# One fused rotation, attention and quantised-FFN kernel: six short steps put in other places of VectorE's, ScalarE's and TensorE's queues

## The reference, cut to what matters

```
a, ang = amplitudes ** dt, frequencies * dt          # one pair per sequence and feature
x' = rotate(x; a*cos(ang), a*sin(ang))
q, k, v = x' @ W_qkv.T (16 heads of 16); k = layernorm(k)
S = gamma_h * S + v_t k_t^T; y_t = S q_t             # decaying linear attention over the 64 tokens
x1 = x + y @ W_o.T
s = tanh(x1 @ W1 + b1) @ v                           # one score per token
p = softmax(masked s over the 64 tokens), mask by the sequence's type
pooled = (p @ x1) / count of unmasked tokens
g = clip(round(pooled / sx)), weights rounded to 8 bits by the largest |w| of each row
out = x1 + dequant(round(silu(g @ Wg) * (g @ Wu)) @ Wd)
```

## Time and profile before

| | us |
|---|---|
| median of 3 runs (275.56 to 279.0) | 275.73 |
| the profiled execution | 275.67 |
| its span in the trace | 273.9 |
| TensorE busy (matmuls) | 254.1 (93%) |
| VectorE busy | 226.4 (83%) |
| ScalarE busy | 183.3 (67%) |
| GpSimd busy | 145.9 (53%) |

### The profile page before, as it was taken

How to read it: one execution, slowest core, us unless ns; L and a number is a source line. 1 busy time by engine, 2 the same in 40 slices (tenths; PEclk the granted TensorE clock), 3 DMA queues, 4 the chain that set the end, 5 groups by cost and what they waited for, 6 DMA issues and landing times.

```text
span 273.9 us, 8463 instructions
## 1 busy us (share of the span) xinstructions
PE 254.1 (93%) x3529; PEld 174.6 (64%) x3529; DVE 226.4 (83%) x483; ACT 183.3 (67%) x325; POOL 145.9 (53%) x144
## 2 busy tenths in 40 slices
PE   5799999989799799989999999998989999998994
PEld 5568788679578677957977977875634434443331
DVE  4879678499779958995996876888888999999994
ACT  5796463562369557858768358437699999838991
POOL 6998693871790395069169233005012779850570
PEclk9999999999999999999999999999999999999999
DMA  5991306204400800390291142040009489000277
GB/s 161 347 276 42 117 2 222 91 0 175 138 2 2 278 33 2 122 244 6 56 288 26 33 146 39 9 149 6 0 34 183 114 221 366 7 0 0 80 257 279
DMA packets 30310, 31.20 MB, mean 114 GB/s; under 512 B 12928, under 2 KB 20672, under 8 KB 30272
## 3 DMA queue, kind: packets, MB, share of 16 engines
q1 hardware_dynamic: 30272, 30.66, 37.4%
HBM read 19.48 MB, written 8.42 MB: 102 GB/s over the span
## 4 chain that ended last, share of the span: by engine, by line
PE 53%; DVE 26%; ACT 12%; issue 5%; DMA 1%; POOL 1%; DVEq 0%; ACTq 0%
PE psum L901 10%; PE psum L1290 6%; DVE arena L1461 5%; PE psum L941 4%; PE psum L1309 3%; PE psum L926 3%; PE psum L1062 3%; ACT silu L864 2%; PE psum L1008 2%; PE psum L1068 2%; PE psum L1063 2%; PE psum L1064 2%; PE psum L1069 2%; ACT silu L846 2%; PE psum L1051 2%
## 5 line engine op out<-in xcount | busy, mean ns | idle before, releaser
L1461 DVE TENSOR_TENSOR arena<-psum,xq_mem 128x512 f32<-128x512 f32 x64 | 39.6, 681 | 3.8 <-PE psum L926 3.7
L560 POOL TENSOR_TENSOR xT_lo<-arena,xT 128x512 fp32r<-128x512 f32 x14 | 17.5, 1273 | 45.4 <-ACT xT L689 45.4
L1290 PE MATMUL psum<-xq_mem,guT 128*128 128x512 bf16 x152 | 33.9, 379 | 0.2
L1290 PEld LDWEIGHTS psum<-xq_mem,guT 128*128 128x128 bf16 x152 | 14.3, 98 | 19.4 <-DVE arena L1675 1.8
L1686 DVE TENSOR_REDUCE h_max<-arena 128x1 f32<-128x1024 f32 (+1 forms) x24 | 25.9, 1123 | 0.2
L846 ACT ACTIVATE silu<-psum,gu_x 128x1024 f32<-128x1024 f32 (+1 forms) x24 | 24.4, 1026 | 2.1 <-PE psum L1290 1.1
L689 ACT ACTIVATE xT<-arena 128x512 fp32r<-128x512 f32 x14 | 8.1, 623 | 22.6 <-PE psum L901 20.9
L941 PE MATMUL psum<-arena 64*32 64x128 f32 x1024 | 19.4, 274 | 1.5 <-DVE arena L1461 1.5
L671 ACT ACTIVATE arena<-psum,pmask 128x512 f32<-128x512 f32 x32 | 20.2, 684 | 0.4 <-PE psum L1069 0.4
L1309 PE MATMUL psum<-arena,dT 128*128 128x512 bf16 x80 | 18.9, 380 | 1.2 <-DVE arena L1745 0.6
L926 PE MATMUL psum<-arena 32*64 32x128 f32 x1024 | 19.7, 278 | 0.1
(11 more groups left out here) (247 smaller groups left out, 721.4 us busy)
## 6 DMA issues: line engine op xcount, KB each, us to landing
arena<-in_x SPq DMA_DIRECT2D x9, 512.0 KB, 3.8
x_dram<-arena SPq DMA_DIRECT2D x8, 512.0 KB, 4.0
pooled<-x_dram SPq DMA_DIRECT2D x8, 512.0 KB, 5.3
out<-pooled SPq DMA_DIRECT2D x15, 256.0 KB, 2.1
xin<-in_x_t SPq DMA_DIRECT2D x7, 512.0 KB, 4.4
cs_rows<-cs_dram SPq DMA_DIRECT2D x12, 256.0 KB, 5.3
pooled<-in_w_qkv_t SPq DMA_DIRECT2D x3, 256.0 KB, 5.0
pooled<-in_w_down SPq DMA_DIRECT2D x1, 704.0 KB, 7.8
```

What stands on the lines that cost most here:

```text
L560: pool.tensor_tensor(xT_lo[:, k, :], xrotT[:, k, :], xT[:, k, :].bitcast(F32), ALU.subtract).then_inc(xl_ok, 1)
L1290: mm = pe.matmul(in_order(o[:, 512 * half:512 * half + 512], 2 * n + half), gT[i][:, v, c, :], xq_rows(2 * n + half, c), start=(c == 0), s ...
L1461: dve.tensor_tensor(dec[:, c, r, :, :], bank[S_BANK[r]].rearrange("q (n k) -> q n k", n=PP), two_heads, ALU.mult).then_inc(dec_done, 1)
```

## The change

Six edits, all of order or of place:

1. VectorE: `scale_v` of each group stands behind `softmax_weights`, `scales` and the clip factors instead of ahead of them.
2. VectorE: `gu_largest(0)` of group 1 stands ahead of `softmax_scores` (it stood behind `sums_copy`); `gu_largest(1)` and `down_largest` of groups 2 and 3 stand ahead of `sums_copy` (they stood behind it).
3. ScalarE writes the first 8 columns of sine and cosine to PSUM (banks 2 and 3) and the other 24 to SBUF: four activations instead of two; VectorE's L1398 and L1399 read them in PSUM; the other columns' products wait for `trig_ok` at 4.
4. TensorE: the turn of the cosine table stands behind `scores(0, 0)` instead of ahead of `squares(0, 0)`, and goes to bank 2.
5. ScalarE: the copy to `cs_T` stands behind both pairs of query copies and both exponents. `hidden_weights` waits for it instead of `scores(0, 0)`.
6. TensorE's matmuls without a use at the start (`keep_clock`) write bank 0 instead of bank 3.

```diff
@@ ScalarE, start
-            act.activation(ang[:, 4, :], ang[:, 2, :], ACT.Sin).then_inc(trig_ok, 1)
-            act.activation(ang[:, 5, :], ang[:, 3, :], ACT.Sin).then_inc(trig_ok, 1)
+            first, rest = slice(0, 2 * PP), slice(2 * PP, NPAIR)
+            act.activation(bank[2][:, first], ang[:, 2, first], ACT.Sin).then_inc(trig_ok, 1)
+            act.activation(bank[3][:, first], ang[:, 3, first], ACT.Sin).then_inc(trig_ok, 1)
+            act.activation(ang[:, 4, rest], ang[:, 2, rest], ACT.Sin).then_inc(trig_ok, 1)
+            act.activation(ang[:, 5, rest], ang[:, 3, rest], ACT.Sin).then_inc(trig_ok, 1)
@@ ScalarE, ahead of the loop
-            act.wait_ge(cs_tr, 1)
-            act.activation(cs_T[:, :], bank[4][0:2 * NPAIR, 0:P], ACT.Copy).then_inc(csT_ok, 1)
             for c in range(DC):
                 q_copies(0, c)
                 act.wait_ge(dec_arg, c + 1)
                 act.activation(decay[:, HC * c:HC * c + HC, :], ..., ACT.Exp).then_inc(dec_exp, 1)
+            act.wait_ge(cs_tr, 1)
+            act.activation(cs_T[:, :], bank[2][0:2 * NPAIR, 0:P], ACT.Copy).then_inc(csT_ok, 1)
@@ TensorE
             def scores(g, c):
-                    pe.wait_ge(csT_ok, 1)
             def hidden_weights():
+                pe.wait_ge(csT_ok, 1)
-            pe.wait_ge(cs_ok, 2)
-            pe.wait_ge(csr_ok, 2)
-            pe.transpose(bank[4][0:2 * NPAIR, 0:P], cs[:, :, :]..., ident[:, :]).then_inc(cs_tr, 1)
             squares(0, 0)
...
                 scores(g, 0)
                 if g == 0:
+                    pe.wait_ge(cs_ok, 2)
+                    pe.transpose(bank[2][0:2 * NPAIR, 0:P], cs[:, :, :]..., ident[:, :]).then_inc(cs_tr, 1)
                     pe.wait_ge(wl_ok, 2)
@@ VectorE, start
-            dve.tensor_tensor(cs[:, 1, first], a_pow[:, first], ang[:, 4, first], ALU.mult)
-            dve.tensor_tensor(cs[:, 0, first], a_pow[:, first], ang[:, 5, first], ALU.mult).then_inc(cs1_ok, 1)
+            dve.tensor_tensor(cs[:, 1, first], a_pow[:, first], bank[2][:, first], ALU.mult)
+            dve.tensor_tensor(cs[:, 0, first], a_pow[:, first], bank[3][:, first], ALU.mult).then_inc(cs1_ok, 1)
...
             dve.wait_ge(pow_ok, 2)
+            dve.wait_ge(trig_ok, 4)
@@ VectorE, loop over g
                 decays(g, 0)
-                for p in range(PP) if g else (2, 3, 0, 1):
-                    scale_v(g, p)
                 if 2 <= g < G - 1:
                     softmax_weights(c - 1)
...
                 elif g == G - 1:
                     softmax_weights(c - 1)
+                for p in range(PP) if g else (2, 3, 0, 1):
+                    scale_v(g, p)
...
                 decays(g, 1)
...
+                if g == 1:
+                    gu_largest(0)
                 if g:
                     softmax_scores(c)
...
                     softmax_sums(c)
-                    sums_copy(g + 1)
-                    if g < 3:
-                        gu_largest(g - 1)
+                    if g == 2:
+                        gu_largest(1)
                     elif g == 3:
                         down_largest()
+                    sums_copy(g + 1)
                     y_odd(g, 0)
```

More of the change, by code:

```diff
@@ L1097, in project_v @@
                               v_mm if p % 2 else None, False)
-            keep_clock(14, bank[3][:, 0:P], ident[:, :], ident[:, :])
+            keep_clock(14, bank[0][:, 0:P], ident[:, :], ident[:, :])
             pe.wait_ge(cs1_ok, 1)
@@ L1109, in _ @@
                 last.then_inc(xT_tr, 1)
-                keep_clock(1, bank[3][:, 0:P], ident[:, :], ident[:, :])
+                keep_clock(1, bank[0][:, 0:P], ident[:, :], ident[:, :])
             pe.wait_ge(wk_ok, 1)
@@ L1126, in _ @@
             project_x(0, Q_BANK, 0, 0, q_mm)
-            pe.wait_ge(cs_ok, 2)
-            pe.wait_ge(csr_ok, 2)
-            pe.transpose(bank[4][0:2 * NPAIR, 0:P], cs[:, :, :].rearrange("p k n -> p (k n)"), ident[:, :]).then_inc(cs_tr, 1)
             squares(0, 0)
@@ L1144, in _ @@
                 if g == 0:
+                    pe.wait_ge(cs_ok, 2)
+                    pe.transpose(bank[2][0:2 * NPAIR, 0:P], cs[:, :, :].rearrange("p k n -> p (k n)"), ident[:, :]).then_inc(cs_tr, 1)
                     pe.wait_ge(wl_ok, 2)
```

## The result

| | before | after |
|---|---|---|
| median, us | 275.72 (4 runs) | 268.0 (4 runs, 267.99 to 268.05) |
| ratio of after to before | | 0.971, 95% interval 0.9669 to 0.975 |
| span in the trace, us | 273.9 | 266.3 |

The change makes the kernel 7.7 us faster. The forecast was 268.6, in 267.0 to 271.8. Some executions are longer at a lower granted clock (the kernel before ran up to 279.0 us here, and in the first experiments six of its 17 took about 278.7 at 0.987 or 0.988), and the ratios still contain such ones, so that they can differ by 0.3% from what the medians give.

The account below looks back on a forecast made before the run. The prediction took TensorE to bound the kernel, with 6.07 us of holes in groups 1 to 4 from late VectorE and other steps. Loop 6.4, cosine turn 0.5 and sines 0.2 made 7.1: 275.67 to 268.6 us, range 267.0 to 271.8.

Parts of the forecast that it names:

- Total: Whole kernel: loop, cosine turn and sines in PSUM together save 7.1 us, giving 268.6 us.
- Sum of the loop: Groups 1 to 4: 5.8 us from holes that go, 6.6 from groups as dense as group 5; 6.4 taken.
- its upper way: Loop estimate in which groups 1 to 4 become as dense as group 5: 6.6 us.
- Edit 1, hold and gap: VectorE's softmax steps, 0.9 us, fit the 1.08 us before L560; TensorE's 1.64 us hole goes in groups 2 and 3.
- Edit 1, cover of `scale_v`: In group 2 `scale_v` ends at 68.95, TensorE's pooling wants it at 69.9: 0.95 us to spare.
- Edit 2 and "the two edits are worth their sum only together": Moved maxima remove `yT` waits: 0.89 us in group 1, 0.4 and 0.25 in 2 and 3; otherwise earlier TensorE waits longer.
- Cosine turn: At the start, moving TensorE's cosine turn behind the scores takes 0.56 us off the path; gain 0.5, between 0.2 and 0.6.
- Sines in PSUM: At the start, L1398 falls from 0.95 to 0.15 us, but L1406 is held by GpSimd's casts; gain 0.2 us.
- A: TensorE meets another wait (held softmax steps, late `scale_v` or `yT`): 271.8 us, or 270.2 with three quarters kept; chance 0.21.
- B: GpSimd isn't the cause and VectorE's long operations stay long; only maxima and start count: 274 us; chance 0.07.
- C: L560 starts ahead of the softmax steps even in the new order, holding VectorE and delaying `scale_v`: 278 us; chance 0.04.
- D: Groups 1 to 4 fall under the forecast floor and L1406 isn't held: 267 us; chance 0.06.

Follow-up runs that it names:

- the first experiments: Follow-up runs made after the change was measured, each with the kernel before run beside it; its medians there were 276.13, 275.68 and 275.61 us.
- old_order_late_low: Kernel before, VectorE order untouched, with GpSimd's L560 of groups 2 to 6 waiting until that group's softmax weights are made: 271.21 us, 271.27 in a second trace.
- scale_v_late: Changed kernel with two unread 128x1024 reductions ahead of `scale_v` in groups 2 to 6: 272.88 us.
- only_order: Kernel before with only the softmax steps and scales moved ahead of `scale_v`: 271.3 us.
- only_maxima: Kernel before with only the weight maxima moved into other VectorE gaps: 269.8 us.
- rot_psum: Changed kernel with ScalarE's half of the rotation of group 0 also in PSUM, leaving L1408 one SBUF operand: 267.32 us.
- maxima_slip: Kernel before with only the maxima moved, plus one unread reduction ahead of the softmax steps in groups 2 and 3: 272.26 us.

## Why the prediction was right, step by step

**Total: right.** Forecast 7.1 us, measured 7.7. It came from TensorE's busy time in each group, and the groups did become that dense.

**Sum of the loop: right, at its upper way.** The dense pattern of group 5 gave 6.6, and 6.63 was measured; the mean of 6.4 was a needless discount. The forecast windows of 20.5, 22.2, 22.2 and 21.2 became 20.41, 22.17, 22.17 and 21.26.

**Edit 1, hold and gap: right.** The steps have 0.15 and 0.43 us; L1569 ends 0.83 us after `decays` hand over, where 0.9 was forecast. L1453 (L1456 in the changed kernel), the one feared to be caught, runs in 0.17 us at 64.43, 0.7 ahead of L560. The gap had grown from 1.08 to 1.49 us, since VectorE reaches the decays 1.19 us into the group instead of 1.61, while L560 stays at 5.08. The cause, GpSimd's L560, was argued from end times in the prediction; `old_order_late_low` shows it.

**Edit 1, cover of `scale_v`: right in kind, under-sized.** 0.95 us was forecast; `scale_v` ends at 66.13 and the pooling starts at 67.73, 1.6 us. Of the difference, 0.4 is VectorE's earlier entry and 0.24 that the steps and scales delay `scale_v` by 1.06 us (63.68 to 64.74), where the working had 1.3. `scale_v_late` found the waits where they were expected.

**Edit 2 and "the two edits are worth their sum only together": wrong.** This is the step that failed. I had priced edit 2 with the arrival of VectorE at L1559 left as it was, so each edit had its own hole. But edit 2 moves that arrival, and L1559 had missed L560 by a few tenths. Alone it gives 5.9, not the 1.5 to 1.9 of the `yT` holes, and the two overlap by 3.7 us, about 1.2 in each of groups 2 to 4. Nor did the reason given hold: with edit 1 alone the waits for `yT` were to grow, and stayed at 0.89, 0.41 and 0.27 us. The total didn't suffer, because it was also worked out from a floor, TensorE's busy time, which doesn't ask which edit fills which hole.

**Cosine turn: right.** 0.5 forecast, 0.6 measured as a difference (1.00 less 0.37). The squares start at 16.83, where 17.1 was forecast. The later store cost nothing: it went out at 21.20 (21.8 forecast), and L398 behind it in the queue was issued at 25.00, 0.33 earlier than before. GpSimd's rotation of group 2, which waits for the table, starts at 31.40 instead of 30.82, but it starts at 31.19 and 31.29 in `only_order` and `only_maxima` too, where the turn is in its old place. It ends at 39.3, and ScalarE reads it at 44.05. TensorE shows no wait at `hidden_weights`.

**Sines in PSUM: right in kind, under-sized.** 0.2 forecast, 0.37 measured, within the -0.1 to 0.75 stated. The product was unheld as forecast, and the casts took back the rest: the row of eight starts 0.87 earlier and ends 0.35 earlier. How they did it was not as worked out: the first L1408 was to be held up to both casts, and seven more of 0.26 us from 10.1 end at 11.9, not at the 11.8 of the working, which would have left no gain. In fact the first ran ahead of the casts (8.68), the second (8.95) between them and the third (9.56) behind them, so that five were left where seven had been expected. `rot_psum` gave 0.7 more.

**Rivals.** A and B didn't come about. C's point, where L560 starts ahead of the steps in the new order, wasn't reached and wasn't run; `scale_v_late` measured only its second half, a late `scale_v`. D's figure of 267 is nearly that of `rot_psum`, which takes the hold off L1408; the groups went to the forecast floor, not under it. What remains of the holes is group 1's 0.25 us for `xT_lo`.

## What to carry to other kernels

When a tiny VectorE operation lasts a microsecond, look at what GpSimd runs at that moment and at how many SBUF operands both have; then move either of the two, or put one operand in PSUM. Price edits that act on one engine's timing by the floor of the stage as well as one by one, for gains shared between them don't add. An order of arrival that is decided by hundredths of a microsecond should be made safe by program order, even where it happens to be favourable.

## What the runs showed of the hardware

- A held VectorE operation shows no idle time ahead of it: it appears as busy, 1.05 us for four columns that take 0.15. Whoever looks for idle time alone misses it.
- The `tensor_scalar` of six columns from SBUF to SBUF (L1453) was held too, at 1.23 us in `only_maxima` against 0.17 unheld, while the inverse L1563 ran in 0.18 us beside L560 in `maxima_slip`. The Trainium skill (page "SBUF — State Buffer", section "Who interferes with whom") has both: two-port modes are in conflict with GpSimd, an instruction outside them with one SBUF input isn't. The trace agrees in the times; it doesn't show in which mode an instruction ran.
- The hold goes both ways. GpSimd's casts, with a single input, took 0.76 and 0.67 us beside the rotation row with two SBUF operands and 0.61 and 0.62 once that had one. Two of the L1408 lasted 0.69 us where 0.34 is the usual. In `only_maxima` the second L560 of group 2 lasted 1.45 us instead of 1.27, while L1566 (66.55 to 67.73) ran past its start at 67.41.
- The switch is sharp: a start of L1559 0.03 us ahead of L560 (`only_maxima`) and one 0.18 us behind it (`maxima_slip`) differ by 0.96 us in a single operation (0.15 against 1.11), in groups 2 and 3 alike.
